# Products with the inverse on eight tiles of the array, the second batch's results turned by half of the partitions

## The chip, the cores and the metric

One core of a Trainium2 chip runs the whole program. The time is the device time of one execution in microseconds. TensorE is called PE here, its weight loads PEld, VectorE DVE, ScalarE ACT, GpSimd POOL, SyncE SP.

## What is computed

A block of a network on `x` of shape [2, 4096, 512]: layer norm, then the sum of `x`, a delta-rule attention of 16 heads of width 32, and a gated FFN (512 to 1536 to 512).

```python
def step(S, inp):                                  # 4096 tokens, one after the other
    qt, kt, vt, bt = inp
    v_pred = jnp.einsum('bhk,bhkv->bhv', kt, S)
    delta = (vt - v_pred) * bt[..., None]
    S = S + kt[..., None] * delta[:, :, None, :]
    ot = jnp.einsum('bhk,bhkv->bhv', qt, S)
    return (S, ot)
...
xn = _layernorm(x, axis=-1)
x = x + _L0_attn_ref(xn, ...) + _L0_ffn_ref(xn, ...)
```

## The kernel before, in words

The recurrence is done in chunks of 32 tokens. Inside a chunk a 32 x 32 triangular system stands for the steps; its inverse is made once, and two products with it, called w (from the keys) and u (from the values), turn the recurrence over chunks into a few small matmuls. The 4096 tokens of both batches are walked in 16 **spans** of 256 tokens (`SPANS`, `TURNS`); a span has 8 chunks, 2 batches and 16 heads, that is 256 problems of 32 x 32. Four heads lie one under the other on the 128 partitions, 32 partitions each, so there are 64 groups of four problems. `quads` (L351) issues four matmuls for a group, one for each quarter h of the partitions: weights and moving data from partitions 32h, result to partitions 32h of a bank of PSUM. In the 32 x 32 tiles of the array these are the four on the diagonal. In float32 each of them is two instructions in the trace.

A span, in the order of PE's program, is: projections of q, k, v and beta with the grams of the keys between them (`project`, `gram`); the output projection of the span before (`project_out`); seventeen gate/up halves of the FFN (`gate_up`, L440, eight matmuls of 512 columns each); then the **products with the inverse** (L530 to L543); then the recurrence over 8 chunks, two groups of tile matmuls in each. Gate/up and down matmuls are put between the tile matmuls as filling, by hand: ten behind each pair of the products (`FILL_UW`), seven behind each half of a chunk (`FILL_CHAIN`).

The products with the inverse are eight steps g, each of eight groups n: `quads` with weights `tt` (the transposed inverse, tile mt, read with a step of 32 elements) and as moving data the keys and values of the problem (`kpv[:, 1:3]`, 64 columns), into bank `T[g % 4]`. After each step `tiled_done` rises by one, and after each odd g come ten filling matmuls.

- DVE, `read_w(g)` (L1217 to L1221): waits for step g of `tiled_done`, transposes the w half of the bank in 32 x 32 blocks into `kq`, and raises `w_ready`. Between these reads its queue, written by hand (L1287 to L1309), has `low_part` (L1184, tile f_lo), `fuse_tile` (L1191), and the statistics of the next span's layer norm (L894). Ahead of them `t_transposed` (L1215, tile mt) makes the transposed inverse, behind a chain of 62 dependent operations (`row_products`, `off_rows`).
- ACT, `copy_u(g)` (L723 to L727): waits for `w_ready` of g, so that DVE and ACT never read a bank together, copies the u half into `vt` (tile kpv), and raises `u_ready`.
- PE: steps 4 to 7 reuse the four banks, so step g waits for copy g - 4 (`u_ready`). The recurrence's first matmuls (L545 to L557) wait for all eight of `w_ready` and `u_ready`.

In `kq`, `vt` and the state a head's data stay on the quarter of the partitions that the head has everywhere else.

Of the kernel before, what the change touches and what calls it, by code (L numbers as in the profile page):

```python
# [6 lines left out]
HEADS, DH = 16, 32  # L7
INNER = 1536
P = 128
# [89 lines left out]
def delta_block_kernel(nc: bass.Bass, x: bass.AP, wq: bass.AP, wk: bass.AP, wv: bass.AP, wb: bass.AP,  # L99
# [11 lines left out]
    with ctx:  # L111
# [154 lines left out]

        def at_span(it, turn, per_span, n=0, turns=TURNS):

            return it * (turns * per_span) + (turn * per_span + n)
# [80 lines left out]
        def _(pe):  # L350
            def quads(out, lhs, rhs, start=True, shared=False):  # L351

                for h in range(QUADS):
                    s = slice(32 * h, 32 * h + 32)
                    last = nc.tensor.matmul(out[s], lhs[s], rhs[s], start=start, stop=True, skip_group_check=shared)  # L355
                return last
# [28 lines left out]
            def all_spans(it=0):  # L385
                for turn in range(TURNS):
# [143 lines left out]
                    for g in range(8):  # L530
                        pe.wait_ge(tt_ready, since(2, g // 4 + 1))
                        if g < 4:
                            pe.wait_ge(m_ready, since(2, 2))
                            pe.wait_ge(p_ready, since(2, 2))
                        else:
                            pe.wait_ge(u_ready, since(8, g - 3))
                        pe.nop(nofuse=True)
                        for n in range(8):
                            pc = 8 * g + n
                            last = quads(T[g % 4][:, 64 * n:64 * n + 64], tt[:, pc // 32, :, pc % 32], kpv[:, 1:3, pc * DH:(pc + 1) * DH])  # L540
                        last.then_inc(tiled_done, 1)
                        if g % 2:
                            fill(fill_uw(g // 2), FILL_UW)  # L543
# [35 lines left out]
        def _(act):  # L579
# [49 lines left out]
            def all_spans(it=0):  # L629
                for turn in range(TURNS):  # L630
# [92 lines left out]
                    def copy_u(g):  # L723
                        act.wait_ge(w_ready, since(8, g + 1))
                        nc.scalar.activation(vt[:, 8 * g:8 * g + 8, :],
                                             T[g % 4][:, :].rearrange("p (n a d) -> p n a d", n=8, a=2)[:, :, 1, :],
                                             ACT.Copy).then_inc(u_ready, 1)  # L727
# [164 lines left out]
        def _(dve):  # L892
# [140 lines left out]
            def all_spans(it=0):  # L1033
                for turn in range(TURNS):
# [182 lines left out]
                    def read_w(g):  # L1217

                        dve.wait_ge(tiled_done, since(TILED, DONE_UW + g + 1))
                        nc.vector.transpose(kq[:, 8 * g:8 * g + 8, 0, :],  # L1220
                                            T[g % 4][:, :].rearrange("p (n a d) -> p n a d", n=8, a=2)[:, :, 0, :]).then_inc(w_ready, 1)  # L1221
# [197 lines left out]
```

## Time and profile before

| | |
|---|---|
| median of 3 runs | 2374.27 us (2373.99 to 2375.14) |
| the profiled execution, its own time | 2373.19 us |
| its span in the profile | 2371.5 us |
| busy: PE, DVE, ACT, POOL | 2263.0, 1787.3, 862.5, 265.4 us |
| mean granted clock of PE, of full speed | 0.988 |

The busy time of an engine is the time in which at least one of its instructions ran. A span of 256 tokens repeats every 142.6 us or so, and the stage with the products is some 17 us of it. Times in rows are microseconds from the start of the profile's span; the granted clock (PEclk) is 1.00 at 2.4 GHz and 0.50 at 1.2 GHz. PE's busy time counts each matmul until its modelled end, so neighbours overlap.

### The profile page before, as it was taken

What the parts mean: (1) busy time and instruction counts of PE and PEld (TensorE: products, weight loads), DVE (VectorE), ACT (ScalarE), POOL (GpSimd) and SP (SyncE); (2) the same over time, 40 slices, a digit from 0 to 9 for tenths busy, and PEclk for the clock granted to TensorE, in tenths of its full rate; (3) what the DMA queues carried; (4) which work ended last, traced back from release to release, by engine and by line L of the source; (5) the groups of instructions that cost most, each with busy time, mean ns of one, the idle gap of its engine ahead of it and who ended that gap; (6) DMA issues with size and microseconds to landing.
All of it is one profiled execution on the core that took longest, in us unless ns stands there. A gap on an engine that the chain in (4) does not pass through costs nothing.

```text
span 2371.5 us, 89650 instructions
## 1 busy us (share of the span) xinstructions
PE 2263.0 (95%) x40688; PEld 1221.6 (52%) x40688; DVE 1787.3 (75%) x3167; ACT 862.5 (36%) x2077; POOL 265.4 (11%) x519
## 2 busy tenths in 40 slices
PE   3889999999999999999999999999999999999996
PEld 1455455555545555455555545555455555545553
DVE  8976968778686776968768686786968768686775
ACT  4652524324242342524325242342423325242341
POOL 2101010010100101010020100101011020100100
PEclk7999999999999999999999999999999999999998
DMA  7000111001111000111001111001111001111000
GB/s 253 19 7 17 37 21 37 16 7 38 21 37 21 29 14 18 37 21 37 16 8 37 21 37 22 26 13 21 37 21 37 12 12 37 21 37 21 11 11 20
DMA packets 89978, 68.96 MB, mean 29 GB/s; under 512 B 68480, under 2 KB 68480, under 8 KB 89600
## 3 DMA queue, kind: packets, MB, share of 16 engines
q1 hardware_dynamic: 88880, 63.20, 9.3%
q8 instruction: 321, 5.26, 0.9%
q14 instruction: 57, 0.47, 0.1%
q10 hardware_dynamic: 720, 0.03, 0.0%
HBM read 30.72 MB, written 16.78 MB: 20 GB/s over the span
## 4 chain that ended last, share of the span: by engine, by line
PE 93%; DVE 5%; issue 1%; DMA 0%; ACT 0%; POOL 0%; SPq 0%; DVEq 0%; POOLq 0%
PE D L440 27%; PE D L430 22%; PE T L355 22%; PE D L506 15%; PE D L371 7%; DVE outer_v L1198 1%; DVE at L1205 0%; DVE f_lo L1184 0%; DVE amax L935 0%; DVE outer_p L1341 0%; DVE state L1343 0%; DVE kq L925 0%; DVE wd L926 0%; DMA xs<-_attn_hidden_states_dram 0%; DVE wgu L926 0%
## 5 line engine op out<-in xcount | busy, mean ns | idle before, releaser
L440 PE MATMUL D<-xt,wgu 128*128 128x512 f16 x3072 | 687.8, 380 | 9.7 <-ACT sg L720 6.4
L430 PE MATMUL D<-xt,w_hi 128*128 128x512 f16 x1664 | 489.6, 381 | 24.6 <-DVE w_lo L978 24.6
L440 PEld LDWEIGHTS D<-xt,wgu 128*128 128x128 f16 x3072 | 290.7, 98 | 357.8 <-ACT sg L720 6.9
L506 PE MATMUL D<-wd,f_hi 128*128 128x512 bf16 x768 | 292.5, 381 | 14.1 <-DVE f_lo L1184 14.1
L506 PE MATMUL D<-wd,f_lo 128*128 128x512 bf16 x768 | 292.5, 381 | 0.0
L430 PE MATMUL D<-xt,w_lo 128*128 128x512 f16 x768 | 292.2, 381 | 0.0
L1205 DVE TENSOR_TENSOR at<-at,outer_v 128x62 f32<-128x62 f32 (+15 forms) x496 | 262.1, 529 | 11.8
L1198 DVE TENSOR_TENSOR outer_v<-mt,at 128x62 f32<-128x62 f32 (+15 forms) x496 | 260.9, 526 | 13.0
L430 PEld LDWEIGHTS D<-xt,w_hi 128*128 128x128 f16 x1664 | 158.9, 98 | 213.4 <-issue 26.9
L710 ACT ACTIVATE kpv<-kpv,rk 128x32 f32<-128x32 f32 x1024 | 231.1, 307 | 1.5
L720 ACT ACTIVATE sg<-D,gs 128x512 f32<-128x512 f32 x192 | 131.6, 685 | 208.9 <-PE D L440 208.9
L772 ACT ACTIVATE qt<-T 128x256 f32<-128x256 f32 x128 | 49.1, 383 | 434.8 <-DVE outer_p L1341 434.8
L1322 DVE STREAM_TRANSPOSE outer_v<-T 128x256 f32<-128x256 f32 x128 | 57.6, 450 | 138.2 <-PE T L355 138.2
L355 PE MATMUL T<-kpv,mt 32*32 32x64 f32 x8192 | 135.0, 220 | 24.8 <-issue 24.8
L884 POOL TENSOR_TENSOR xs<-xs,fuse 128x512 f32<-128x512 f32 x64 | 81.1, 1267 | 687.6 <-DVE fuse L1316 687.6
L355 PEld LDWEIGHTS T<-kpv,mt 32*32 32x32 f32 x8192 | 126.7, 134 | 52.5 <-issue 52.5
L1341 DVE STREAM_TRANSPOSE outer_p<-T 128x256 f32<-128x256 f32 x128 | 57.6, 450 | 125.4 <-PE T L355 125.4
L355 PEld LDWEIGHTS T<-kpv 32*32 32x32 f32 x8192 | 120.3, 105 | 54.5 <-issue 54.2
L355 PEld LDWEIGHTS T<-kq,state 32*32 32x32 f32 x8192 | 120.1, 105 | 54.8 <-issue 54.3
L371 PE MATMUL D<-wo_hi,qt 128*128 128x512 f16 x480 | 142.8, 379 | 0.0
L355 PE MATMUL T<-kq,state 32*32 32x64 f32 x8192 | 141.3, 216 | 0.0
L355 PE MATMUL T<-kpv 32*32 32x64 f32 x8192 | 141.3, 216 | 0.0
(173 smaller groups left out, 2596.4 us busy)
## 6 DMA issues: line engine op xcount, KB each, us to landing
xs<-_attn_hidden_states_dram SPq DMA_DIRECT2D x32, 512.0 KB, 3.5
out_dram<-xs SPq DMA_DIRECT2D x32, 512.0 KB, 3.0
fuse<-in_L_ffn_gate_w_dram SPq DMA_DIRECT2D x2, 768.0 KB, 8.4
xs<-in_L_ffn_up_w_dram SPq DMA_DIRECT2D x2, 768.0 KB, 9.1
f_hi<-in_L_ffn_down_w_dram SPq DMA_DIRECT2D x2, 768.0 KB, 9.9
f_lo<-in_L_ffn_down_w_dram SPq DMA_DIRECT2D x2, 768.0 KB, 11.5
kpv<-in_L_attn_Wk_dram SPq DMA_DIRECT2D x1, 1024.0 KB, 10.8
qt<-in_L_attn_Wq_dram SPq DMA_DIRECT2D x1, 1024.0 KB, 12.9
```

The source lines that it names most:

```text
L355: last = nc.tensor.matmul(out[s], lhs[s], rhs[s], start=start, stop=True, skip_group_check=shared)
L371: ins = nc.tensor.matmul(D[bank][:, :], o_part[:, m, j * P:(j + 1) * P], w[:, m, :], start=n == 0, stop=n == 11)
L430: last = nc.tensor.matmul(D[bank][:, :], w[:, k, cols], xp[:, k, :], start=n == 0, stop=n == len(products) - 1)
L440: last = nc.tensor.matmul(D[bank][:, :], wgu[:, n // 2, c:c + P], (xt_hi, xt_lo)[n % 2][:, n // 2, :], start=n == 0, stop=n == 2 * KT_ - 1)
L506: last = nc.tensor.matmul(D[bank][:, :], (f_hi, f_lo)[n % 2][:, ic, j * P:(j + 1) * P], wd[:, ic, :], start=n == 0, stop=n == 2 * IC - 1)
L710: return nc.scalar.activation(v_problem, v_problem, ACT.Identity, scale=rk[:, n:n + 1])
L720: nc.scalar.activation(sg[:, ic % 2, :], D[bank_of(gate_up_job(2 * ic))][:, :], ACT.Silu, scale=gs[:, ic:ic + 1]).then_inc(sg_ready, 1)
L884: nc.gpsimd.tensor_tensor(xs[:, par, j, :], xs[:, par, j, :], fuse[:, j % 2, :], ALU.add).then_inc(acc_ready, 1)
L1198: solved[0] = step(nc.vector.tensor_tensor(products(j), m_prob[:, :, j, j + 1:].unsqueeze(3).to_broadcast(shape), t_prob[:, :, j, 0:j + 1] ...
L1205: solved[0] = step(nc.vector.tensor_tensor(rest, rest, products(j), ALU.subtract))
L1322: nc.vector.transpose(blocks(outer_v), chain_banks(c)[:, :, :, 0, :]).then_inc(ws_read, 1)
L1341: nc.vector.transpose(blocks(outer_p), chain_banks(c)[:, :, :, 2, :]).then_inc(ds_read, 1)
```

## The change

Pairs of steps are taken together. For each n, `quads` of the even step is followed at once by `quads` of the odd step. In the odd step (g % 2, which is the second batch) the results are **turned**: the matmul with operands on quarter h writes to quarter h ^ 2, so the tiles are those two columns beside the diagonal, and the two batches use eight different tiles. `tiled_done` rises by two at the end of the pair. The wait on `u_ready` is made once for a pair, for the copy that the odd step needs (g - 2 for even g, which is the odd step's g - 3).

The readers of odd steps put the data back: two operations, each reading one half of the partitions and writing the other, in place of one over all 128. That holds for `read_w` on DVE and for `copy_u` on ACT. Filling, banks and the order of DVE's and ACT's queues are as before.

```diff
--- before.py
+++ after.py
@@ -264,6 +264,12 @@
         on_ready, ohi_ready, olo_ready = sem("on_ready"), sem("ohi_ready"), sem("olo_ready")
         v_step, p_step = sem("v_step"), sem("p_step")
 
+        low_half, high_half = slice(0, P // 2), slice(P // 2, P)
+
+        def turned_parts(g):
+
+            return ((low_half, high_half), (high_half, low_half)) if g % 2 else ((slice(0, P), slice(0, P)),)
+
         def at_span(it, turn, per_span, n=0, turns=TURNS):
 
             return it * (turns * per_span) + (turn * per_span + n)
@@ -348,11 +354,12 @@
 
         @block.tensor
         def _(pe):
-            def quads(out, lhs, rhs, start=True, shared=False):
+            def quads(out, lhs, rhs, start=True, shared=False, turned=False):
 
                 for h in range(QUADS):
                     s = slice(32 * h, 32 * h + 32)
-                    last = nc.tensor.matmul(out[s], lhs[s], rhs[s], start=start, stop=True, skip_group_check=shared)
+                    to = slice(32 * (h ^ 2), 32 * (h ^ 2) + 32) if turned else s
+                    last = nc.tensor.matmul(out[to], lhs[s], rhs[s], start=start, stop=True, skip_group_check=shared)
                 return last
 
             def transpose_xn(j, bank):
@@ -527,20 +534,21 @@
                         pe.wait_ge(ffn_ready, 1)
                     pe.wait_ge(kt_ready, since(MS, MS))
                     pe.wait_ge(vk_ready, since(1, 1))
-                    for g in range(8):
+                    for g in range(0, 8, 2):
                         pe.wait_ge(tt_ready, since(2, g // 4 + 1))
                         if g < 4:
                             pe.wait_ge(m_ready, since(2, 2))
                             pe.wait_ge(p_ready, since(2, 2))
                         else:
-                            pe.wait_ge(u_ready, since(8, g - 3))
+                            pe.wait_ge(u_ready, since(8, g - 2))
                         pe.nop(nofuse=True)
                         for n in range(8):
-                            pc = 8 * g + n
-                            last = quads(T[g % 4][:, 64 * n:64 * n + 64], tt[:, pc // 32, :, pc % 32], kpv[:, 1:3, pc * DH:(pc + 1) * DH])
-                        last.then_inc(tiled_done, 1)
-                        if g % 2:
-                            fill(fill_uw(g // 2), FILL_UW)
+                            for b in range(BATCH):
+                                pc = 8 * (g + b) + n
+                                last = quads(T[(g + b) % 4][:, 64 * n:64 * n + 64], tt[:, pc // 32, :, pc % 32],
+                                             kpv[:, 1:3, pc * DH:(pc + 1) * DH], turned=b == 1)
+                        last.then_inc(tiled_done, 2)
+                        fill(fill_uw(g // 2), FILL_UW)
 
                     for c in range(STEPS):
 
@@ -722,9 +730,10 @@
 
                     def copy_u(g):
                         act.wait_ge(w_ready, since(8, g + 1))
-                        nc.scalar.activation(vt[:, 8 * g:8 * g + 8, :],
-                                             T[g % 4][:, :].rearrange("p (n a d) -> p n a d", n=8, a=2)[:, :, 1, :],
-                                             ACT.Copy).then_inc(u_ready, 1)
+                        made = T[g % 4][:, :].rearrange("p (n a d) -> p n a d", n=8, a=2)
+                        for to, src in turned_parts(g):
+                            last = nc.scalar.activation(vt[to, 8 * g:8 * g + 8, :], made[src, :, 1, :], ACT.Copy)
+                        last.then_inc(u_ready, 1)
 
                     act.wait_ge(k_norm_ready, since(1, 1))
                     act.wait_ge(v_ready, since(MS, MS))
@@ -1217,8 +1226,10 @@
                     def read_w(g):
 
                         dve.wait_ge(tiled_done, since(TILED, DONE_UW + g + 1))
-                        nc.vector.transpose(kq[:, 8 * g:8 * g + 8, 0, :],
-                                            T[g % 4][:, :].rearrange("p (n a d) -> p n a d", n=8, a=2)[:, :, 0, :]).then_inc(w_ready, 1)
+                        made = T[g % 4][:, :].rearrange("p (n a d) -> p n a d", n=8, a=2)
+                        for to, src in turned_parts(g):
+                            last = nc.vector.transpose(kq[to, 8 * g:8 * g + 8, 0, :], made[src, :, 0, :])
+                        last.then_inc(w_ready, 1)
 
                     def add_out(j):
```

On PE, in the stage with the products, steps 4 to 7 of a span stood so (L355 is `quads`, L440 the filling; T is the bank, mt the transposed inverse, kpv keys and values):

```order
L355 MATMUL T<-kpv,mt 32x64 [waits tt_ready,u_ready]
L355 MATMUL T<-kpv,mt 32x64 x31
L355 MATMUL T<-kpv,mt 32x64 [waits tt_ready,u_ready]
L355 MATMUL T<-kpv,mt 32x64 x31
L440 MATMUL D0<-xt,wgu 128x512 x4
L440 MATMUL D1<-xt,wgu 128x512 [waits sg_ready]
L440 MATMUL D1<-xt,wgu 128x512 x5
L355 MATMUL T<-kpv,mt 32x64 [waits tt_ready,u_ready]
L355 MATMUL T<-kpv,mt 32x64 x31
L355 MATMUL T<-kpv,mt 32x64 [waits tt_ready,u_ready]
L355 MATMUL T<-kpv,mt 32x64 x31
L440 MATMUL D1<-xt,wgu 128x512 x2
```

and now stand so (the lines have moved on by seven):

```order
L362 MATMUL T<-kpv,mt 32x64 [waits tt_ready,u_ready]
L362 MATMUL T<-kpv,mt 32x64 x63
L447 MATMUL D0<-xt,wgu 128x512 x4
L447 MATMUL D1<-xt,wgu 128x512 [waits sg_ready]
L447 MATMUL D1<-xt,wgu 128x512 x5
L362 MATMUL T<-kpv,mt 32x64 [waits tt_ready,u_ready]
L362 MATMUL T<-kpv,mt 32x64 x63
L447 MATMUL D1<-xt,wgu 128x512 x2
```

Two runs of 32 matmuls with a wait each have become one run of 64 with one wait; the filling is the same.

On DVE, in the same stage, the reads of steps 4 to 7 (kq is written, T read) with what lies between them stood so:

```order
L1220 STREAM_TRANSPOSE kq<-T 128x8x32
L1184 TENSOR_TENSOR f_lo<-qt,f_hi 128x512
L1220 STREAM_TRANSPOSE kq<-T 128x8x32
L1191 SCALAR_TENSOR_TENSOR fuse<-D0,usf,sg 128x512
L1184 TENSOR_TENSOR f_lo<-qt,f_hi 128x512
L894 BN_STATS stats<-xs 128x6 x2
L1220 STREAM_TRANSPOSE kq<-T 128x8x32
L894 BN_STATS stats<-xs 128x6 x2
L1220 STREAM_TRANSPOSE kq<-T 128x8x32
```

and now:

```order
L1231 STREAM_TRANSPOSE kq<-T 128x8x32
L1193 TENSOR_TENSOR f_lo<-qt,f_hi 128x512
L1231 STREAM_TRANSPOSE kq<-T 64x8x32 x2
L1200 SCALAR_TENSOR_TENSOR fuse<-D0,usf,sg 128x512
L1193 TENSOR_TENSOR f_lo<-qt,f_hi 128x512
L903 BN_STATS stats<-xs 128x6 x2
L1231 STREAM_TRANSPOSE kq<-T 128x8x32
L903 BN_STATS stats<-xs 128x6 x2
L1231 STREAM_TRANSPOSE kq<-T 64x8x32 x2
```

Each second read is two instructions on 64 partitions.

## Rows read from the trace of the kernel before

**Rows 1.** The page, part 4: the chain that ended last, by engine.

```profile
PE 93%; DVE 5%; issue 1%; DMA 0%; ACT 0%; POOL 0%; SPq 0%; DVEq 0%; POOLq 0%
```

**Rows 2.** Timeline of PE, eighth span: start us, us, engine, line, operation, count, [idle before].

```profile
1138.65 2.09 PE L355 MATMUL T<-kpv,mt 32*32 32x64 f32 x128 [1.26 <-issue]
1140.67 2.33 PE L440 MATMUL D<-xt,wgu 128*128 128x512 f16 x10
1142.93 2.10 PE L355 MATMUL T<-kpv,mt 32*32 32x64 f32 x128
...
1151.49 2.08 PE L355 MATMUL T<-kpv,mt 32*32 32x64 f32 x128
1153.51 2.33 PE L440 MATMUL D<-xt,wgu 128*128 128x512 f16 x10
1155.77 1.09 PE L355 MATMUL T<-kq,state 32*32 32x64 f32 x64
```

**Rows 3.** Groups of instructions by line: the T matmuls, their loads, the two readers.

```profile
L355 PE MATMUL T<-kpv,mt 32*32 32x64 f32 x8192 | 135.0, 220 | 24.8 <-issue 24.8
...
L355 PEld LDWEIGHTS T<-kpv,mt 32*32 32x32 f32 x8192 | 126.7, 134 | 52.5 <-issue 52.5
...
L1220 DVE STREAM_TRANSPOSE kq<-T 128x256 f32<-128x256 f32 x128 | 56.7, 443 | 52.4 <-PE T L355 52.4
...
L725 ACT ACTIVATE kpv<-T 128x256 f32<-128x256 f32 x128 | 49.1, 383 | 165.2 <-DVE kq L1220 165.2
```

**Rows 4.** Timeline of DVE in the same stage.

```profile
1137.19 2.37 DVE L1215 STREAM_TRANSPOSE mt<-at 128x1024 f32<-128x1024 f32 x2
1139.85 0.45 DVE L1220 STREAM_TRANSPOSE kq<-T 128x256 f32<-128x256 f32 x1 [0.29 <-PE T L355]
1140.23 0.65 DVE L1184 TENSOR_TENSOR f_lo<-fuse,f_hi 128x512 f16<-128x512 f32 x1
1140.80 0.45 DVE L1220 STREAM_TRANSPOSE kq<-T 128x256 f32<-128x256 f32 x1
1141.17 1.25 DVE L1184 TENSOR_TENSOR f_lo<-fuse,f_hi 128x512 f16<-128x512 f32 x2
...
1145.46 0.71 DVE L1191 SCALAR_TENSOR_TENSOR fuse<-D,usf,sg 128x512 f32<-128x512 f32 x1
...
1151.57 1.28 DVE L894 BATCH_NORM_STATS2 stats<-xs 128x6 f32<-128x512 f32 x2
1152.77 0.43 DVE L1220 STREAM_TRANSPOSE kq<-T 128x256 f32<-128x256 f32 x1
...
1154.28 0.43 DVE L1220 STREAM_TRANSPOSE kq<-T 128x256 f32<-128x256 f32 x1
1154.64 0.65 DVE L1184 TENSOR_TENSOR f_lo<-fuse,f_hi 128x512 f16<-128x512 f32 x1
```

**Rows 5.** Timeline of ACT at the end of the stage.

```profile
1154.75 0.38 ACT L725 ACTIVATE kpv<-T 128x256 f32<-128x256 f32 x1 [1.13 <-DVE kq L1220]
1155.03 0.68 ACT L720 ACTIVATE sg<-D,gs 128x512 f32<-128x512 f32 x1
```

**Rows 6.** Windows: busy time of PE, PEld, DVE, ACT, POOL (instructions), then PEclk, DMA.

```profile
1138.65:1155.77 17.12, 17.12 (x552) 11.38 (x552) 13.51 (x29) 5.48 (x12) 0.04 (x1) 1.00 0.02 4
```

**Rows 7.** Timeline of PE in the first span: three pauses.

```profile
104.91 3.31 PE L440 MATMUL D<-xt,wgu 128*128 128x512 f16 x8 [6.41 <-ACT sg L720]
109.98 3.63 PE L440 MATMUL D<-xt,wgu 128*128 128x512 f16 x16 [1.76 <-DVE fuse L1191]
...
138.90 3.41 PE L355 MATMUL T<-kpv,mt 32*32 32x64 f32 x128 [5.89 <-issue]
```

**Rows 8.** Windows of two microseconds in the first span, columns as in rows 6.

```profile
108.00:110.00 2.00, 0.24 (x3) 0.02 (x2) 1.97 (x4) 0.04 (x1) 0.00 (x0) 1.00 0.94 321
...
134.00:136.00 2.00, 0.00 (x0) 0.00 (x0) 1.86 (x6) 2.00 (x7) 0.00 (x0) 0.78 0.00 0
...
140.00:142.00 2.00, 2.00 (x88) 2.00 (x84) 1.02 (x2) 0.38 (x1) 0.00 (x0) 0.52 0.03 8
```

## The prediction

> **What bounds the kernel now.** I read the chain of waits first: PE holds 93% of it and DVE 5% [rows 1]. The span is one period of about 142.6 us repeated 16 times, so one period is enough, and of it the stage that the diff touches: the products with the inverse, from 1138.65 to 1155.77 in the eighth span. The timeline of PE shows four equal pairs there, each 128 tile matmuls, followed by ten gate/up matmuls; a pair with its ten takes 4.28 us (1138.65 to 1142.93) and nothing is idle until the recurrence begins at 1155.77 [rows 2]. PE is busy for all of the 17.12 us, DVE for 13.51, ACT for 5.48 [rows 6]. So the stage is bound by PE, with a second limit at 79% of it. The 1.26 us of idle ahead of the stage belongs to DVE: the two transposes of the inverse start at 1137.19, and the matmuls follow the first of them [rows 2, 4]. The change touches neither, so the start of the stage stands still and everything is counted from it (0 = 1138.65).
>
> **What a pair costs.** Ten gate/up matmuls take 2.33 us with the tail of the last, which is 0.38; nine steps of 0.217, so ten are 2.17. The pair itself is 4.28 - 2.17 = 2.11. It is 32 rounds of four tiles: (2.09 - 0.22)/32 = 58 ns a round [rows 2, 3]. A load of 134 ns and a matmul of 220 ns [rows 3] fit in rounds of 58 only if they overlap, so a round's length is the time that one tile's row of the array streams or loads, not a latency.
>
> **1. Alternation.** The second batch's matmuls go from rows h to columns h+2, so eight different tiles take turns and none is asked for twice within eight matmuls. Bounds from the trace: below, two rounds of four run as one of 58 ns, which makes 16 rounds, 0.93 us off a pair (2.11 to 1.18); above, no overlap, 2.11. The trace has no matmul off the diagonal. I take 1.18, since a round is paced by one tile's turn and the eight are distinct. It leaves PE 7 ns per matmul (58/8) where it has 14.6 now (1.87/128); no row shows such a rate sustained.
> "LDWEIGHTS overlaps with in-flight MATMULs only when row_grp differs", says the Trainium skill ("TensorE: Matmul & The Clock Gate", Part 3). Both batches use the same row groups, so by that rule the pair stays at 2.11; the trace leans against it, since a load of 134 ns hides in 58 ns rounds on the very same rows.
>
> **2. The readers.** Every odd g is read by two operations on 64 partitions where one on 128 was, on DVE and on ACT, four times a span. The free size per partition is the same, so each half costs what the whole did. On DVE the next operation starts 0.37 to 0.38 after a transpose, though it lasts 0.44 [rows 3, 4]. No row has an operation that reads one half of the partitions and writes the other. Bounds for the two: 2 x 0.375 = 0.75, if they overlap as usual, and 2 x 0.44 + 0.08 = 0.96, if each runs to its end and the one before it too. I take 0.96 (0.59 more than now): these change both where they read and where they write, and the duration is the nearer row.
> The Trainium skill's "VectorE: DVE Perf Modes", section "Two Vector instructions with no wait between them", gives a model by which an instruction whose start quadrant differs from the last one's waits until all earlier ones finish. By it the cost is the 0.96; without it, 0.75, and each span would gain some 0.6 us more.
> On ACT one copy lasts 0.38 and the next starts 0.28 after it [rows 5]; two take 0.66 to 0.76, I take 0.70.
>
> **3. The signal.** Both tiles of a pair are announced together. Now the first is read at 1.20 (1139.85), which is half a pair plus 0.15 [rows 4]. With a pair of 1.18 it is 1.33; without overlap 2.26. The stage's later waits on u_ready ask for copies 1 and 3 at once; both are made long before.
>
> **The sum of a span.** DVE's queue in the order of the code, with the steps of rows 4 (f_lo 0.57 to 0.60, fuse 0.65, a pair of statistics 1.20, whole transpose 0.38, split 0.96): transpose 0 at 1.33, f_lo, transpose 1 done 3.24, two f_lo to 4.44; tiles 2, 3 are there at 3.35 + 1.33 = 4.68; then 0.38, 0.57, 0.96, 0.63, 1.21 give 8.43 (tiles 4, 5 are there at 8.03); 0.38, 0.57, 0.96, 0.66, 0.60 and the first statistics 1.20 give 12.80 (tiles 6, 7 at 11.37); 0.38, 1.16, 0.96 give 15.30 for the last transpose. The copy (0.04 + 0.70) and PE's start behind a semaphore (0.2; the first T matmul begins at 1138.65, 0.24 behind the first transpose's end, 1137.19 + 1.22) bring the recurrence to 16.2, against 17.12 now. **DVE becomes the bound**: PE has done its four pairs and fills at 4 x 3.35 = 13.4 and then waits 2.8 us for w_ready and u_ready. Of 3.7 us that the matmuls save, 0.9 are left, 14.7 us over 16 spans. What DVE does next (f_lo, 1154.64 today) has room ahead of the recurrence's first read.
>
> **4. The clock.** The pause of 2.8 us is new, and must be priced. In the first span the granted clock was 1.00 (2.4 GHz) behind a pause of 1.76 us [rows 7, 8]. In the pause of 5.89 us it fell: 0.78 from 134 to 136, so to half (1.2 GHz) at 135.1, 2.1 us after the last matmul (138.90 - 5.89 = 133.01). It came back at 141.9 (0.52 from 140 to 142), after 3.0 us of work at half the clock: there 128 tile matmuls took 3.41 instead of 2.09, and after the pause of 6.41 eight gate/up matmuls 3.31 instead of 1.9 [rows 7]. Half of 3.0 is 1.5 us lost; here more of the slow stretch is work, I take 1.6. A pause of 2.8 lies above both 1.76 and 2.1, so I let it fall in 14 of 16 spans (bounds 0 and 16): 22.4 us. The recurrence behind it has PE as its bound, so nothing hides that.
>
> Total: -14.7 + 22.4 = +7.7 on the profiled execution's 2373.19, 2380.9. The median of the runs, 2374.27, lies 1.1 above it: **2382.0**.
>
> **The rivals.**
> A: *no overlap* on the same rows. The pair stays 2.11; tiles 6 and 7 are there at 3 x 4.28 + 2.11 + 0.15 = 15.1, then 0.38, 1.16, 0.96 on DVE, 0.74 on ACT and 0.2: 18.5, 1.4 later than now, 22 us in all: 2397 (2393 with the cheap split). For it: the quoted rule, and that no off-diagonal tile is in the trace.
> B, on the other side: *the clock holds*. The matmuls overlap, the pause does no harm, and the 14.7 us are a gain: 2359.5. With split transposes of 0.75 the pause is 2.2 us and the gain near 24: 2350. It decides at the pause: at 2.1 us or less the clock can't have fallen, above it each span that keeps its clock is worth 1.6 us. For it: 1.76 was harmless, and both falls seen were in pauses over twice as long.
> C: *half an overlap*, with PE's queue or the loads as the limit: a pair of 1.5 to 1.7. By the same queue the recurrence starts 0.3 earlier to 0.2 later, and the pause is about 2 us and taken as harmless: 2370 to 2378, which may not be told from no change.
>
> **How the numbers follow.** Forecast (overlap, DVE bound, clock falls) 0.34; A 0.23; B 0.28; C 0.15. A measurement of this kernel tells about 0.2%, 4.7 us, from no change. The forecast spreads over 2370 to 2387 with the number of falls and the split's price: three quarters of it slower, a fifth same. Faster: B, a little of C and of the forecast, 0.34. Same: 0.16. Slower: 0.50. Range: 2356 to 2398 holds the forecast, C, most of A and B's dear half; below lies the cheap split with a steady clock.
>
> **What would show it.** A pair of T matmuls in 1.1 to 1.3 us instead of 2.09 (step 1); two transposes of 0.44 with the next start 0.96 after the first (2); PE idle for 2.5 to 3 us ahead of the recurrence behind ACT's copy at L735 (sum); granted clock below 1.00 in the 3 to 4 us behind that pause in most spans (4). A pair near 2.1 makes A right and the forecast wrong; a clock of 1.00 throughout makes it B.

## The result, and the profile after

| | before | changed |
|---|---|---|
| median of 9 runs each | 2375.01 us | 2380.61 us (2379.17 to 2382.89) |
| ratio | | 1.0024, interval 1.0014 to 1.0034 |
| profiled span, mean granted clock | 2371.5 us, 0.988 | 2378.7 us, 0.986 |

The changed kernel is slower by 0.24%, 5.6 us, which is little more than the 4.7 us that the prediction took for the least that can be told from no change. The total came within 1.4 us of the forecast. The page's chain of waits by engine shows that the bound has moved a little from PE to DVE, where 93% and 5% stood before [rows 1]:

```profile
PE 84%; DVE 11%; issue 4%; ACT 0%; DMA 0%; POOL 0%; SPq 0%; DVEq 0%; POOLq 0%
```

The timeline of PE in the eighth span, to be laid beside [rows 2]:

```profile
1142.37 1.59 PE L362 MATMUL T<-kpv,mt 32*32 32x64 f32 x128 [1.26 <-issue]
1143.89 2.33 PE L447 MATMUL D<-xt,wgu 128*128 128x512 f16 x10
1146.15 1.59 PE L362 MATMUL T<-kpv,mt 32*32 32x64 f32 x128
...
1155.24 2.33 PE L447 MATMUL D<-xt,wgu 128*128 128x512 f16 x10
1159.69 1.10 PE L362 MATMUL T<-kq,state 32*32 32x64 f32 x64 [2.11 <-ACT kpv L735]
```

A pair with its ten takes 3.78 us (1142.37 to 1146.15) where 4.28 stood. By the working of the prediction the pair is 3.78 - 2.17 = **1.61 us** (2.11 before). That is the usual pair: behind the first span 13 of 61 are longer, 1.65 to 1.76 us in their rows where 1.59 stands here. In rounds it is (1.59 - 0.22)/32 = 43 ns for four matmuls, not the 58 of before and not the 29 of the forecast. The four pairs gave back 2.0 us, and PE then waits 2.11 us for ACT's copy. The recurrence starts 17.32 us into the stage, **0.20 later** than before. DVE in the same stage, beside [rows 4]:

```profile
1143.99 0.45 DVE L1231 STREAM_TRANSPOSE kq<-T 128x256 f32<-128x256 f32 x1 [0.71 <-PE T L362]
1144.37 0.65 DVE L1193 TENSOR_TENSOR f_lo<-fuse,f_hi 128x512 f16<-128x512 f32 x1
1145.05 0.91 DVE L1231 STREAM_TRANSPOSE kq<-T 64x256 f32<-64x256 f32 x2
1145.99 1.29 DVE L1193 TENSOR_TENSOR f_lo<-fuse,f_hi 128x512 f16<-128x512 f32 x2
1147.78 0.45 DVE L1231 STREAM_TRANSPOSE kq<-T 128x256 f32<-128x256 f32 x1 [0.50 <-PE T L362]
...
1156.45 1.25 DVE L903 BATCH_NORM_STATS2 stats<-xs 128x6 f32<-128x512 f32 x2
1157.72 0.91 DVE L1231 STREAM_TRANSPOSE kq<-T 64x256 f32<-64x256 f32 x2
1158.66 0.69 DVE L1193 TENSOR_TENSOR f_lo<-fuse,f_hi 128x512 f16<-128x512 f32 x1
```

DVE waits only for the first two pairs (0.71 and 0.50 us); from 1147.78 on it is never idle, up to the last split at 1157.72. The reader that ACT runs behind it, and the window of the whole stage (columns as in rows 6):

```profile
1158.66 0.77 ACT L735 ACTIVATE kpv<-T 64x256 f32<-64x256 f32 x2 [1.73 <-DVE kq L1231]
```

```profile
1142.37:1159.69 17.32, 15.21 (x553) 9.43 (x554) 15.78 (x32) 6.62 (x16) 0.00 (x0) 1.00 0.02 4
```

PE went from 17.12 busy of 17.12 to 15.21 of 17.32, DVE from 13.51 to 15.78 [rows 6]. The wait is in every span: the waits of the whole execution have it 16 times (total, count, the longest), which is 1.88 to 2.13 in each of the first 15 spans and 0.27 in the last:

```profile
PE T L362 <- ACT kpv L735: 30.9, 16, 2.1
```

**The clock behind the pause.** In 4 of the first 15 spans it fell. This is the span before the one shown, on PE's timeline and in windows of two microseconds:

```profile
1015.33 1.27 PE L362 MATMUL T<-kq,state 32*32 32x64 f32 x64 [2.12 <-ACT kpv L735]
1016.53 3.14 PE L447 MATMUL D<-xt,wgu 128*128 128x512 f16 x7
1019.60 1.10 PE L362 MATMUL T<-kpv 32*32 32x64 f32 x64
```

```profile
1014.00:1016.00 2.00, 0.68 (x49) 0.71 (x53) 1.62 (x8) 1.44 (x3) 0.57 (x1) 1.00 0.00 0
1016.00:1018.00 2.00, 2.00 (x35) 0.93 (x24) 1.17 (x3) 0.00 (x0) 0.82 (x2) 0.52 0.04 8
1018.00:1020.00 2.00, 2.00 (x32) 0.69 (x34) 0.45 (x1) 0.63 (x1) 0.00 (x0) 0.62 0.01 4
1020.00:1022.00 2.00, 2.00 (x59) 1.13 (x47) 1.20 (x3) 0.75 (x2) 0.00 (x0) 1.00 0.00 0
```

The recurrence's first burst starts after a pause of 2.12 us, and the granted clock was at half (1.2 GHz) from 1016.1 to 1019.5, so it fell when PE had been at work again for 0.8 us; seven gate/up matmuls took 3.14 us there and 1.69 at the full clock. From the recurrence to the next pair such a span takes 127.0 us instead of 125.4 (1.6 more; once 2.3), and a whole period 144.3 to 145.1 instead of 142.65 to 143.13 (the first span, 144.58, aside).

**The balance of the spans**, from the starts of the recurrence and of the periods in both traces: later recurrences in 15 spans +3.0, the way from there to the next period +7.1 (the four periods with a fall +7.3, the other eleven -0.2), the last span -1.6 (its recurrence starts at 15.51, since DVE has no statistics of a next span to make), what is behind that -1.4, the start +0.15. That makes the +7.2 of the profiled spans.

### The profile page after: what moved, and what is told of

Same layout as the page of the kernel before. It is cut to its first block, busy times and chain, and to the rows that moved or that the text cites. A ratio compares the mean times of both kernels' runs of the same rounds, so it can differ in the third digit from the quotient of the medians.

```text
span 2378.7 us, 89458 instructions
## 1 busy us (share of the span) xinstructions
PE 2205.3 (93%) x40464; PEld 1193.7 (50%) x40688; DVE 1826.0 (77%) x3231; ACT 888.1 (37%) x2141; POOL 265.8 (11%) x519
## 4 chain that ended last, share of the span: by engine, by line
PE 84%; DVE 11%; issue 4%; ACT 0%; DMA 0%; POOL 0%; SPq 0%; DVEq 0%; POOLq 0%
PE D L447 23%; PE D L437 22%; PE T L362 19%; PE D L513 13%; PE D L378 7%; DVE f_lo L1193 2%; DVE kq L1231 2%; DVE stats L903 1%; DVE fuse L1200 1%; DVE outer_v L1207 1%; DVE at L1214 0%; DVE amax L944 0%; DVE outer_p L1352 0%; DVE state L1354 0%; ACT kpv L735 0%
## 5 line engine op out<-in xcount | busy, mean ns | idle before, releaser
L513 PE MATMUL D<-wd,f_hi 128*128 128x512 bf16 x656 | 248.9, 379 | 31.9 <-issue 17.8
L513 PE MATMUL D<-wd,f_lo 128*128 128x512 bf16 x656 | 248.8, 379 | 16.1 <-issue 15.3
L735 ACT ACTIVATE kpv<-T 64x256 f32<-64x256 f32 (+1 forms) x192 | 72.9, 380 | 170.5 <-DVE kq L1231 169.8
L362 PEld LDWEIGHTS T<-kq 32*32 32x32 f32 x8192 | 117.9, 105 | 27.7 <-issue 27.7
```

The costliest lines, as they stand in the source:

```text
L362: last = nc.tensor.matmul(out[to], lhs[s], rhs[s], start=start, stop=True, skip_group_check=shared)
L513: last = nc.tensor.matmul(D[bank][:, :], (f_hi, f_lo)[n % 2][:, ic, j * P:(j + 1) * P], wd[:, ic, :], start=n == 0, stop=n == 2 * IC - 1)
L735: last = nc.scalar.activation(vt[to, 8 * g:8 * g + 8, :], made[src, :, 1, :], ACT.Copy)
```

## The experiments

Each edit is made on the changed kernel unless it says otherwise. "Recurrence" is its start counted from the first pair of its span, "pause" PE's idle time ahead of it. All kernels have a pause of over 5 us ahead of the first span's stage; the fall behind that one is left out of every count. A repeated number such as the start of the recurrence is that of the usual span. e2, e3, e4 and e7 compute other results than the network's, which the text says at each.

### Matmuls and readers apart: three of four corners

**e1, alternation on the old tiles.** All of the new order and signal, but the second batch on the diagonal and read whole.

```diff
-            return ((low_half, high_half), (high_half, low_half)) if g % 2 else ((slice(0, P), slice(0, P)),)
+            return ((slice(0, P), slice(0, P)),)
...
-    kpv[:, 1:3, pc * DH:(pc + 1) * DH], turned=b == 1)
+    kpv[:, 1:3, pc * DH:(pc + 1) * DH], turned=False)
```

> The changed kernel's order of matmuls (both batches in alternation, one signal for a pair), but every result on the diagonal tiles and the readers whole, as before. Theory 'tiles' (the gain of a pair comes from the eight distinct tiles): a pair is back at 2.1 us; tiles 6 and 7 are there at 15.1 us of the stage, and 0.38 + 1.16 + 0.38 on DVE, 0.42 on ACT and 0.2 to start put the recurrence at 17.6 instead of 17.13, so 7 us over before: about 2382. Theory 'order' (issuing two banks in turn is what shortens a pair, whatever the tiles): a pair near 1.6, the recurrence at about 15.6, 2350. The granted clock stays at 1.00, since PE pauses for 0.5 us at most.

Measured: 2379.65 us, ratio 1.0027 (1.0017 to 1.0038).

```profile
1141.81 2.08 PE L362 MATMUL T<-kpv,mt 32*32 32x64 f32 x128 [1.26 <-issue]
...
1159.42 1.10 PE L362 MATMUL T<-kq,state 32*32 32x64 f32 x64 [0.44 <-ACT kpv L735]
```

The pair stays at 2.08: order alone overlaps nothing, the eight tiles do. What is left is the price of the joint signal, a recurrence at 17.61 (0.49 later than before), with no fall.

**e2, whole readers on the turned results.** Only the first line of the edit above. The second batch's heads then lie in the wrong half: the halves are not turned back.

> The changed kernel with turned matmuls, but read_w and copy_u read odd steps whole, without turning them back, so the second batch's w and u come from the wrong heads. Theory 'readers' (the split reads are what eats the gain): pairs stay at 1.59, the recurrence starts at 15.6 instead of 17.32, the pause falls from 2.1 to about 0.45 us, no fall of the clock behind it, about 24 us under before: 2350. Rival 'the queue of DVE was full anyway, and the late signal costs as much as the pair saves': the recurrence at 17 or later, 2372 to 2376.

Measured: 2349.67 us, ratio 0.9902 (0.9885 to 0.9918).

```profile
986.80 1.59 PE L362 MATMUL T<-kpv,mt 32*32 32x64 f32 x128 [1.26 <-issue]
...
1002.43 1.09 PE L362 MATMUL T<-kq,state 32*32 32x64 f32 x64 [0.42 <-ACT kpv L735]
```

With a pair of 1.59 and no split, the recurrence starts at 15.63 (up to 16.33 in other spans) and the pause is 0.42; the clock doesn't fall. So the turned matmuls with their joint signal are worth 23.7 us, and turning the halves back costs all of that and 5.6 more.

**e7, the split alone.** Only the second line of the first edit: the matmuls stay on the diagonal, the readers are split and turn halves that need no turning.

> The changed kernel with all products on the diagonal tiles but the readers split as in the change (so the second batch's halves end up exchanged): the cost of the readers and the signal without the gain of the pairs, which is rival A of the prediction in kind. Pairs 2.08 us; the recurrence starts at 18.7 (tiles 6 and 7 at 15.1, then 0.38 + 1.2 + 0.94 on DVE, 0.04 + 0.77 on ACT, 0.2), 1.55 us later than before: 23 to 25 us over before, 2397. With the run on the same tiles with whole readers (6 us over) it gives the split's price alone: about 18 us. If that price is under 10 us, something other than the split held DVE in the change.

Measured: 2396.76 us, ratio 1.0096 (1.0080 to 1.0111).

```profile
1162.08 2.08 PE L362 MATMUL T<-kpv,mt 32*32 32x64 f32 x128
...
1168.00 1.10 PE L362 MATMUL T<-kq,state 32*32 32x64 f32 x64 [1.58 <-ACT kpv L735]
```

The first pair of that span starts at 1149.26, so the recurrence at 18.74, without a fall behind the 1.58. This is rival A acted out, and its forecast was 2397. Against each one's own before, the corners are:

| | whole readers | split readers |
|---|---|---|
| diagonal tiles, in alternation | e1: +6.3 us | e7: +22.2 us |
| eight tiles | e2: -23.7 us | the change: +5.6 us |

The split costs 16 us beside slow pairs, where DVE still waits for the first three pairs of a stage, and 29 beside fast ones, where it waits for two, the four falls included.

### What a pair of 1.6 us is bound by

**e3, dense weights.** The loads read 32 contiguous numbers per partition, of another tensor: the products are not those with the inverse.

```diff
-                                last = quads(T[(g + b) % 4][:, 64 * n:64 * n + 64], tt[:, pc // 32, :, pc % 32],
+                                last = quads(T[(g + b) % 4][:, 64 * n:64 * n + 64], mt[:, pc * CHUNK:(pc + 1) * CHUNK],
```

> The changed kernel with the weights of the products read from 32 neighbouring elements of mt instead of elements 32 apart, so the products are of other matrices. A pair takes 1.59 us, 43 ns for four matmuls, where 29 were forecast. Theory 'loads' (the spaced weights of two tiles on the same row group share one path): a pair falls to 1.0 to 1.25. Theories 'streams' and 'queue' (moving data, or PE's rate of instructions): it stays at 1.5 to 1.6. The time moves little, since DVE sets the start of the recurrence: 2375 to 2383.

Measured in one run: 2381.13 us.

```profile
1153.92 1.47 PE L362 MATMUL T<-kpv,mt 32*32 32x64 f32 x128
...
1160.00 1.16 PE L362 MATMUL T<-kq,state 32*32 32x64 f32 x64 [2.34 <-ACT kpv L735]
1161.09 3.17 PE L447 MATMUL D<-xt,wgu 128*128 128x512 f16 x7
```

A load fell from 137 to 104 ns on average, but the pair only to 1.47 (39 ns per four). The pause grew to 2.34, and 8 spans of 15 had a fall; this is one of them.

**e4, half the columns.** Each matmul streams 32 columns instead of 64; the other half of the results isn't computed.

```diff
-                                last = quads(T[(g + b) % 4][:, 64 * n:64 * n + 64], tt[:, pc // 32, :, pc % 32],
-                                             kpv[:, 1:3, pc * DH:(pc + 1) * DH], turned=b == 1)
+                                last = quads(T[(g + b) % 4][:, 64 * n:64 * n + 32], tt[:, pc // 32, :, pc % 32],
+                                             kpv[:, 1:2, pc * DH:(pc + 1) * DH], turned=b == 1)
```

> The changed kernel with 32 moving columns instead of 64 in the products (only the w half is computed, the u half is left out). Theory 'streams': a pair falls from 1.59 to about 0.9 to 1.1. Theories 'loads' and 'queue': it stays at 1.5 to 1.6. Time 2375 to 2383, for the same reason.

Measured in one run: 2379.63 us.

```profile
1009.17 1.48 PE L362 MATMUL T<-kpv,mt 32*32 32x32 f32 x128
...
1015.25 1.52 PE L362 MATMUL T<-kq,state 32*32 32x64 f32 x64 [2.32 <-ACT kpv L735]
```

A pair of 1.48, and 7 spans of 15 had a fall. Halving the stream is worth as little as the dense load, about 0.12 us; neither alone sets the length. No run has both with the pair's own work.

**e6, a probe.** Ahead of the first pair of each span 128 extra matmuls with a dense weight and 32 columns on the four diagonal tiles, ahead of the second the same on eight; both are overwritten by the pairs. (The granted clock fell at 892.1, so the rows from there to 895.5 are at half of it; both extra bursts ran at the full clock.)

```diff
+                        for n in range(8) if g in (0, 2) else ():
+                            for b in range(BATCH):
+                                quads(T[g + (b if g == 2 else 0)][:, 64 * n:64 * n + 32], causal[:, :],
+                                      kpv[:, 1:2, (8 * (g + b) + n) * DH:(8 * (g + b) + n + 1) * DH], turned=b == 1 and g == 2)
```

> The changed kernel with 64 quads' worth of extra matmuls ahead of the first and the second pair of a span (128 matmuls in the trace each), results overwritten by the real ones: small ones, 32 moving columns and weights from 32 neighbouring elements, the first burst on the four diagonal tiles only, the second on the eight. Theory 'queue' (behind the first 30 or so matmuls, which stand ready in PE's queue, instructions come at some 10 ns per matmul with its load): both bursts take 1.4 to 1.5 us, as the pairs with dense weights and with half the columns did (1.47, 1.48), though the first has half the tiles. Theory 'tiles' (a tile's turn is the limit): the first takes 0.9 to 1.3, and the second clearly less than the first.

Measured in one run: 2497.64 us.

```profile
888.08 1.24 PE L362 MATMUL T<-kpv,causal 32*32 32x32 f32 x126 [1.26 <-issue]
889.15 0.25 PE L362 MATMUL T<-kpv,mt 32*32 32x64 f32 x1
...
892.08 1.06 PE L362 MATMUL T<-kpv,mt 32*32 32x64 f32 x51 [1.86 <-issue]
...
896.53 1.25 PE L362 MATMUL T<-kpv,causal 32*32 32x32 f32 x126
897.60 0.26 PE L362 MATMUL T<-kpv,mt 32*32 32x64 f32 x1
...
900.35 0.89 PE L362 MATMUL T<-kpv,mt 32*32 32x64 f32 x62 [1.82 <-issue]
```

On four tiles the next kind starts 1.07 us after the first (888.08 to 889.15), on eight also 1.07 (896.53 to 897.60): 8.3 ns a matmul (128 of them; two stand between the first of the pair and aren't in the x126), whatever the number of tiles. On four tiles all spans but the first give this number; on eight it is 1.06 to 1.08 in eight spans and longer in the others, up to 1.82. So with small matmuls a limit shows that the number of tiles doesn't set, 33 ns for four, near the 39 of e3 and e4. Which limit it is isn't shown. It can be the rate at which matmuls with their loads reach the array. But both bursts use the same four row groups, and a limit in what a row group takes in would give the same two times; no run spreads such matmuls otherwise.

And in each burst of 256 (128 extra ones and the pair) PE stopped once, for 1.2 to 2.5 us, with "issue" as what it waited for: in this span for 1.86 us after 205 matmuls and for 1.82 after 194. **The place of the stop is fixed in the program.** From span to span it moves by three matmuls, 190, 193, 196 and so on up to 235 in the first burst, 179 to 224 in the second. Counted over all that PE executes in the trace in order of time (loads, matmuls and semaphore instructions), the 32 stops are by turns 512 and 5120 instructions apart, multiples of 256 both. So they belong to places in the stream of instructions, and not to the work that stands there.

**v2, each pair in two bursts.** If a store of fetched instructions were drained by a burst of 128, two bursts of 64 with five fillings between would run faster. Made on v1 (below).

```diff
                         for n in range(8):
+                            if n == 4:
+                                fill(fill_uw(g // 2), 5)
...
-                        fill(fill_uw(g // 2), FILL_UW)
+                        fill(fill_uw(g // 2) + 5, FILL_UW - 5)
```

> The version with the statistics later, with each pair in two bursts of 64 matmuls and five filling matmuls between and five behind. Theory 'queue' (only the matmuls that stand ready in PE's queue go at 7 ns, the rest at the rate at which instructions come): each burst has its own 30 ready, so a pair with its ten fillings takes 3.6 instead of 3.79, the recurrence starts 0.3 to 0.5 earlier, 4 to 8 us under the version with one burst: 2340 to 2343. Rival 'tiles' (a round has its length wherever it stands): the extra changes between kinds cost 0.1 to 0.15 each, 6 us over that version: 2353.

Measured: 2379.36 us, ratio 1.0025 (1.0015 to 1.0035).

```profile
1140.86 0.90 PE L362 MATMUL T<-kpv,mt 32*32 32x64 f32 x64 [1.26 <-issue]
1141.69 1.25 PE L447 MATMUL D<-xt,wgu 128*128 128x512 f16 x5
...
1144.90 0.91 PE L362 MATMUL T<-kpv,mt 32*32 32x64 f32 x64
...
1158.42 1.10 PE L362 MATMUL T<-kq,state 32*32 32x64 f32 x64 [1.30 <-ACT kpv L737]
```

The expectation missed. A burst of 64 takes (0.90 - 0.22)/64 = 10.6 ns a matmul, one of 128 (1.59 - 0.22)/128 = 10.7: both halves of a usual pair go at the same rate, though not evenly (in the pair at 1146.15 of the changed kernel 32 matmuls start in 0.29 us, 64 in 0.68, 96 in 1.01). Two edges instead of one make the pair with its ten 4.04 (1140.86 to 1144.90) instead of 3.78, and the fillings between delay the signal; I had left that out. The recurrence went to 17.56. One thing did change: behind the first span v1 has 18 longer pairs in 61, of 1.66 to 1.89 us, and here one burst in 123 is longer than 0.95.

### What the pause does

**e5, the pause filled.** Nine repeats of the first matmul of the next gate/up half, which that half overwrites, behind the last ten; **e8** is the same with four.

```diff
+                            again = take(gate_up_job(22))
+                            for n in range(9):
+                                nc.tensor.matmul(D[again][:, :], wgu[:, 0, 11 * P:12 * P], xt_hi[:, 0, :], start=True, stop=False, skip_group_check=True)
```

> The changed kernel with nine repeats of the next gate/up half's first matmul in the pause ahead of the recurrence. Each repeat starts its sum anew, so the result stays the same; nine take 1.95 us of a pause of 2.1. Theory 'clock' (the falls of the granted clock behind the pause, four in the profiled execution, cost 1.6 to 2.3 us each): the clock never falls in the spans, the recurrence still starts at 17.3, and 5 to 8 us of the time go: within 2 us of before. Rival 'the falls are in the shade of other waits and the loss is all in the later start of the recurrence': no falls either, but the time stays 4 to 6 us over before.

Measured: 2406.84 us, ratio 1.0134 (1.0119 to 1.0150).

```profile
1157.24 1.58 PE L362 MATMUL T<-kpv,mt 32*32 32x64 f32 x126
1160.18 0.27 PE L362 MATMUL T<-kpv,mt 32*32 32x64 f32 x2 [1.35 <-issue]
...
1166.34 2.11 PE L558 MATMUL D<-xt,wgu 128*128 128x512 f16 x9
1168.54 1.10 PE L362 MATMUL T<-kq,state 32*32 32x64 f32 x64
```

There is next to no pause ahead of the recurrence (1166.34 with nine repeats, then 1168.54; 0.16 us at most) and no fall behind it. But neither theory had what came instead: in seven spans, 5 to 11, PE stops in the pairs or their fillings for 0.5 to 1.9 us with no work to wait for, and the recurrence starts at 18.3 to 20.7; in the others it stands at 17.3 to 17.4, the first aside. In spans 5 to 12 PE stops once more, some 95 us behind the first pair, for 0.7 to 2.0 us. Over the whole execution the stops ahead of tile matmuls read

```profile
PE T L362 <- issue: 42.9, 33, 5.9
```

against 25.7 in 19 in the changed kernel; 24.8 in 16 are the pauses ahead of the stages, in this run too. Two of the stops, of 1.86 and 2.02 us, had a fall behind them, at 1452.0 and 1834.3. Behind the first span, periods without such a stop were 142.67 to 143.46. Counted as in e6, all 18 stops of over 0.5 us that aren't ahead of a stage lie at the same place within every 256 instructions (number 193 in 15 cases, 192 in 3), which is also the place of e6's.

**e8, four repeats.** They leave a pause, and PE's queue less to fetch.

> As the run with nine repeats in the pause, with four (0.87 us): the pause falls from 2.1 to about 1.2 us. Theory 'clock': no falls behind the pause, and 5 to 8 us under the changed kernel: within 2 us of before. Theory 'supply' (PE runs out of instructions in the products whenever the time ahead of them doesn't let them come in; nine repeats brought stops of 1.3 to 2 us in the pairs, marked issue): fewer stops than with nine repeats or none, time between 2375 and 2395.

Measured: 2379.04 us, ratio 1.0020 (1.0011 to 1.0029).

```profile
2017.52 1.30 PE L362 MATMUL T<-kq,state 32*32 32x64 f32 x64 [1.25 <-ACT kpv L738]
...
2020.37 1.08 PE L362 MATMUL T<-kpv 32*32 32x64 f32 x58
2021.66 0.31 PE L362 MATMUL T<-kpv 32*32 32x64 f32 x6 [0.21 <-issue]
```

The pause is 1.25 and no span has a fall; the recurrence is at 17.33, as in the change. That part came as the clock theory has it. The total didn't follow: the later spans take 143.1 to 143.8 with small stops like the two here (the first burst 1.30 instead of 1.10, then 0.21 idle), and the whole can't be told from the changed kernel. Both stops are at the place found in e5 and e6 (instructions 193 and 192 of 256). That no falls means no loss is therefore not shown by this run.

### The statistics out of DVE's way

**v1, statistics behind the last transpose.** The first pair of statistics is read behind the last transpose, the second and both aggregations in the first chunk of the recurrence, and two tables put the steps that need them one chunk later.

```diff
-HIGH_AT, LOW_AT = {1: (0, 1), 2: (2, 3)}, {2: 0, 3: 1, 4: 2, 5: 3}
+HIGH_AT, LOW_AT = {2: (0, 1), 3: (2, 3)}, {2: 0, 3: 1, 4: 2, 5: 3}
...
-APPLY_AT, APPLY_LATE = {2: 1}, {0: 0}
+APPLY_AT, APPLY_LATE = {2: 1}, {1: 0}
...
-                    read_statistics(0)
                     read_w(6)
-                    read_statistics(1)
                     read_w(7)
+                    read_statistics(0)
                     low_part(8)
-                    aggregate(0)
-                    aggregate(1)
...
+                        if c == 0:
+                            aggregate(0)
...
+                        if c == 0:
+                            read_statistics(1)
+                            aggregate(1)
```

> The changed kernel with 2.4 us of statistics taken out of DVE's queue ahead of the last reads: read_w(6) and read_w(7) first, the first batch's statistics behind them, the second's and both aggregations in the first chunk, and the layer norm's application and its parts one chunk later. Theory 'DVE's queue sets the start': tiles 6 and 7 are there at 13.1, the last transpose ends at 14.5, the recurrence starts at 15.5 instead of 17.32, the pause is 0.3 us and the clock holds: 24 us under before, 2350, unless what was moved makes PE wait in the recurrence. Rival 'DVE only moves its lateness into the recurrence': the period of a span stays above 142 us, 2370 or more.

Measured: **2346.96 us, ratio 0.9885 (0.9870 to 0.9900)**, faster than both kernels.

```profile
1987.04 1.39 DVE L1231 STREAM_TRANSPOSE kq<-T 128x256 f32<-128x256 f32 x3 [0.45 <-PE T L362]
1988.46 1.29 DVE L903 BATCH_NORM_STATS2 stats<-xs 128x6 f32<-128x512 f32 x2
```

```profile
1989.54 1.10 PE L362 MATMUL T<-kq,state 32*32 32x64 f32 x64 [0.28 <-ACT kpv L735]
```

The last three transposes (a whole one and a split) run without a break, the statistics follow, and DVE has even to wait 0.45 us for the last pair. The recurrence starts at 15.44 in half of the spans, at up to 16.1 in the others; the pause is 0.22, once 0.28, the clock doesn't fall in any span, and periods behind the first are 140.8 to 141.4.

**v1c, the same move on the kernel before**, with the same lines.

> The same move of DVE's work in the kernel before. There PE sets the start of the recurrence (17.13), so by theory 'DVE's queue sets the start only after the change' nothing moves: within 2 us of before. If it gains more than 5 us, the gain of the version with the change is the move's, not the tiles'.

Measured: 2373.75 us, ratio 0.9999 (0.9989 to 1.0008). The recurrence stays at 17.14 behind PE (the first pair of the span starts at 1137.73):

```profile
1154.87 1.10 PE L355 MATMUL T<-kq,state 32*32 32x64 f32 x64
```

So the gain of v1 isn't the move's own: it needs the turned matmuls, and the change lacked only room on DVE to show it.

## Why the prediction came out right

The total was right, and the bound was the forecast one, DVE behind its splits and the statistics. But two terms of the sum were off by a similar amount in opposite directions. The case that came true is nearer to rival C, which had a chance of 0.15, with the forecast's clock in a quarter of the spans.

- **The pair (step 1) is the term that failed.** "Two rounds of four run as one of 58 ns" gave 1.18 us; it is 1.61. The 7 ns a matmul that I had written down as never seen were not reached over a whole burst in any run: 10.7 were measured, and 8.3 in the probe with the smallest matmuls and loads. That is 0.29 on the first signal and 0.43 on the pitch of the pairs, and the second signal holds DVE: 0.72 of the 1.1 us by which the recurrence was later than forecast (17.32 for 16.2).
- **No overlap (rival A) fell.** e1 and e2 differ in the tiles, with the same readers: 2.08 and 1.59. The Trainium skill ("TensorE: Matmul & The Clock Gate", Part 3) says that loads overlap with matmuls in flight only when the row groups differ. Both batches read the same row groups in e1 and in e2, and the pair became shorter by another column group alone; so the 2.11 that the prediction drew from this sentence didn't come, and the measurement decides against it. Whether a load and a matmul of one row group run at the same moment isn't told by the length of a pair.
- **The split (step 2) held, a little dearer.** The step from a split to what follows is 0.94 (1145.05 to 1145.99), for 0.96. The operation ahead of it steps 0.68 instead of 0.57 to 0.60, since it too runs to its end, so that each split costs some 0.66 more than a whole transpose (0.94 - 0.38 for itself, 0.08 to 0.11 for the one ahead) instead of 0.59. The model in the Trainium skill's "VectorE: DVE Perf Modes", "Two Vector instructions with no wait between them", agrees with these rows: an instruction whose start quadrant changes waits for all before it. The three splits after the second signal make 0.26 of the 1.1 us (10.88 from that signal to the end of the last transpose, 1147.78 to 1158.66, where 10.62 were forecast). ACT's two copies take 0.77 for 0.70; with the signals around it 0.1.
- **The signal (step 3)** came with the end of the pair: the first transpose starts 1.62 after the pair, at no distance where I had added 0.15. e1 prices the joint signal without overlap at 0.49 us a span.
- **The sum of a span**: recurrence 0.9 earlier was forecast (-14.7 us in all), 0.20 later came. It cost 3.0 us in 15 spans, and the last span and the end gave 3.0 back: about nothing, instead of -14.7.
- **The clock (step 4)**: the mechanism was right, a fall behind the pause, and the price of one fall too (1.6 us), though the falls began when PE had been at work again for 0.2 to 0.8 us. The count was wrong, 4 instead of 14. The short pairs didn't come, so the pause was 2.11 instead of 2.8; what a pause of 2.8 would have done no run shows. Nor is there the edge at 2.1 on which rival B was to decide: in the changed kernel falls stand behind pauses of 2.04, 2.09, 2.12 and 2.13, and none behind five pauses of 2.11. The falls and the short stops cost 7.1 us instead of 22.4. By the usual pause of each run ahead of the recurrence: 0.4 (e1, e2) no falls, 1.25 and 1.30 (e8, v2) none, 1.58 (e7) none, 2.11 (the change) 4 in 15 spans, 2.32 (e4) 7, 2.34 (e3) 8. More falls go with longer pauses, but in e6 two stops of 2.33 us had none behind them and one of 1.72 had one. C's "harmless at about 2 us" failed at this point, which is why 2380.6 lies above its 2378.

So -14.7 + 22.4 = 7.7 and about 0 + 7.1 = 7.1 agree in part by luck: the short pair that was to gain the time was also to make the long pause that costs the clock, so both were overdone together, but nothing in the steps makes the two sizes equal. Of the other ends, 2397 is where e7 came out, and rival B's 2350 is reached by e2 and v1, once DVE is out of the way.

**What stays open.** What sets the 1.61 us of a usual pair. Loads and streams are worth 0.12 each, and the probe shows 33 ns for four as a limit that isn't the number of tiles, but may be the row groups'; the rest of the 43 ns isn't explained. v2 speaks against a store that the first half of a usual pair drains, not against one behind the longer pairs. The stops at "issue" in e5 and e6 recur at one place in every 256 of PE's instructions, which fits instructions that are brought in by blocks of that size and came late; the bringing itself no trace shows.

## What to carry to other kernels

When a change speeds up the engine that bounds a stage, first lay the next engine's queue against the new dates: here DVE had 3.6 us of room in 17.1, its splits and what they hold up took 2.3 of it while the shorter pairs took 2.0 away, and two pairs of statistics that the recurrence doesn't need stood ahead of the last transpose; moving them was worth 1.4%. Overlap of small matmuls over more tiles is real, but count it by matmuls too, not by tiles alone: here no burst of 128 went faster than 8.3 ns each, on four tiles or on eight. And a new pause on PE is priced twice, once as idle time and once by the granted clock behind it, 1.6 us a fall here.

## What the runs showed of the hardware that was not expected

- PE can stop for up to 2.5 us with nothing to wait for, and it does so at one place in every 256 of its instructions: 0.5 to 2.0 us in e5, 1.2 to 2.5 in each burst of 256 in e6. The same place shows in small. v1 has no such stop beyond those ahead of each stage (24.8 us in 16 waits), but 18 of its pairs are 1.66 to 1.89 us; behind the first 150 us, 19 times more than 0.1 us passes from one load of a run of tile matmuls to the next, and 17 of these are within two instructions of that place, as are 20 of 22 in the changed kernel, 31 of 33 in e8 and 11 of 12 in the kernel before.
- 128 small matmuls with a dense weight take as long on eight tiles as on four, 1.07 us from first start to next kind (both on the same four row groups).
- Whether a pause of about 2 us is followed by a fall isn't told by its length alone. In e4 a pause of 2.41 us had none behind it, one of 2.01 had; the seven falls are all 286.7 us apart, which is two of its spans:

```profile
1588.95 1.77 PE L362 MATMUL T<-kq,state 32*32 32x64 f32 x64 [2.01 <-ACT kpv L735]
```

```profile
1733.17 1.10 PE L362 MATMUL T<-kq,state 32*32 32x64 f32 x64 [2.41 <-ACT kpv L735]
```

  The burst behind the pause shows it: 1.77 us at a clock that is falling, 1.10 at the full one.
- In e8 the falls of the clock were gone and the time stayed: 2379.04 for 2380.61, with small stops in their place.
